# Rounding the feed-forward weights from a turned layout, in two stages instead of one

## The reference, cut to what matters

```python
x = x + _L0_xattn_ref(_layernorm(x, axis=-1), ctx_4096, ...)   # 16 heads of 96, 4 key/value heads, 4352 keys
x = x + _L0_attn_ref(_layernorm(x, axis=-1), ...)
x = x + _L0_ffn_ref(_layernorm(x, axis=-1), ...)
x = x + _L1_xattn_ref(_layernorm(x, axis=-1), ctx_4096, ctx_4096, ...)
x = x + _L1_attn_ref(_layernorm(x, axis=-1), ...)
x = x + _L1_ffn_ref(_layernorm(x, axis=-1), ...)

def _quant_w(W):
    ws = jnp.max(jnp.abs(W), axis=1, keepdims=True) / QMAX
    ws = jnp.maximum(ws, 1e-08)
    Wq = jnp.clip(jnp.round(W / ws), -QMAX, QMAX)
    return (Wq, ws)
...
Wgq, wsg = _quant_w(Wg)     # 2752 x 1024
Wuq, wsu = _quant_w(Wu)     # 2752 x 1024
gate = jnp.einsum('td,id->ti', q, Wgq) * s * wsg.T
up = jnp.einsum('td,id->ti', q, Wuq) * s * wsu.T
h = jax.nn.silu(gate) * up
q2, s2 = _quant_act(h)
Wdq, wsd = _quant_w(Wd)     # 1024 x 2752
out = jnp.einsum('ti,di->td', q2, Wdq) * s2 * wsd.T
```

## Time and profile before

| | us |
|---|---|
| median of 3 runs | 2063.93 (2061.02 to 2064.44) |
| the profiled execution | 2066.84 |
| its span, first to last instruction | 2065.5 |
| latent stage in it | 0 to about 650 |
| cross stage in it | 655 to about 1096 |
| busy over the span | PE 93%, DVE 62%, ACT 42%, POOL 27% |

### The profile page before, as it was taken

How to read it: one execution, slowest core, us unless ns; L and a number is a source line. 1 busy time by engine, 2 the same in 40 slices (tenths; PEclk the granted TensorE clock), 3 DMA queues, 4 the chain that set the end, 5 groups by cost and what they waited for, 6 DMA issues and landing times.

```text
span 2065.5 us, 29644 instructions
## 1 busy us (share of the span) xinstructions
PE 1924.9 (93%) x11932; PEld 1415.2 (69%) x11932; DVE 1279.1 (62%) x1612; ACT 859.0 (42%) x1409; POOL 547.5 (27%) x264
## 2 busy tenths in 40 slices
PE   7899999999997999999999898879999999978988
PEld 5799999999996777878777787533333333366854
DVE  3445454545453778888976764767777775256465
ACT  2211111111111666666565353036676767645431
POOL 0000000000000455555430000136777777610000
PEclk9999999999998999999999999989999999999999
DMA  5533334343324765665644433743343421036033
GB/s 178 175 101 115 109 106 118 98 124 94 84 80 134 212 206 175 203 198 198 220 142 137 162 122 82 168 123 80 73 91 73 87 70 27 21 127 239 1 125 143
DMA packets 154824, 259.30 MB, mean 126 GB/s; under 512 B 36493, under 2 KB 102337, under 8 KB 147521
## 3 DMA queue, kind: packets, MB, share of 16 engines
q1 hardware_dynamic: 154689, 257.42, 41.8%
HBM read 192.39 MB, written 61.76 MB: 123 GB/s over the span
## 4 chain that ended last, share of the span: by engine, by line
PE 82%; DVE 10%; ACT 3%; issue 2%; DMA 2%; SPq 1%; POOL 0%; ACTq 0%; DVEq 0%
PE psum L490 11%; PE psum L1732 7%; PE psum L1749 5%; PE psum L471 4%; PE psum L473 4%; PE psum L472 4%; PE psum L458 4%; PE psum L295 3%; PE psum L296 3%; PE psum L297 3%; PE psum L1765 3%; DVE top L1923 3%; PE psum L438 3%; PE psum L831 3%; PE psum L846 3%; PE psum L833 3%
## 5 line engine op out<-in xcount | busy, mean ns | idle before, releaser
L1923 DVE TENSOR_REDUCE top<-psum 128x4 f32<-128x2048 f32 (+1 forms) x146 | 294.0, 2025 | 97.8 <-PE psum L1713 97.6
L1993 POOL TENSOR_TENSOR added<-probs_f 128x1024 f32<-128x1024 f32 x126 | 299.3, 2377 | 166.3 <-ACT probs_f L1848 118.7
L1848 ACT ACTIVATE probs_f<-psum 128x512 f32<-128x512 f32 x512 | 278.5, 594 | 136.6 <-PE psum L1732 124.1
L623 DVE TENSOR_REDUCE top<-psum 128x2 f32<-128x512 f32 x272 | 186.5, 691 | 198.1 <-PE psum L458 197.9
L922 DVE TENSOR_TENSOR probs_low<-probs,probs_high 128x1024 fp32r<-128x1024 f32 x136 | 196.0, 1445 | 78.8 <-ACT probs L885 78.7
L884 ACT ACTIVATE probs_high<-psum 128x1024 fp32r<-128x1024 f32 x136 | 139.8, 1028 | 165.4 <-PE psum L833 151.8
L1732 PE MATMUL psum<-q_rows,k_rows 97*128 97x512 f32 x512 | 196.0, 457 | 2.7 <-DMA q_rows<-t_high 2.0
L1732 PEld LDWEIGHTS psum<-q_rows,k_rows 97*128 97x128 f32 x512 | 80.0, 189 | 171.8 <-ACT probs_f L1848 161.5
L471 PE MATMUL psum<-c_high,w_high 128*128 128x256 f32 (+1 forms) x672 | 190.7, 284 | 3.2 <-issue 3.2
L472 PE MATMUL psum<-c_low,w_high 128*128 128x256 f32 (+1 forms) x672 | 190.4, 283 | 0.0
L473 PE MATMUL psum<-c_high,w_low 128*128 128x256 f32 (+1 forms) x672 | 190.4, 283 | 0.0
(11 more groups left out here) (363 smaller groups left out, 3814.7 us busy)
## 6 DMA issues: line engine op xcount, KB each, us to landing
wf_rows<-in_ffn_w_dram SPq DMA_DIRECT2D x42, 512.0 KB, 4.1
staged<-in_ctxT_dram SPq DMA_DIRECT2D x32, 512.0 KB, 4.7
k_four<-k_high SPq DMA_DIRECT2D x128, 128.0 KB, 3.3
wf_rows<-in_ffn_w_dram SPq DMA_DIRECT2D x8, 1376.0 KB, 7.6
q_dram<-wf_turned SPq DMA_DIRECT2D x42, 256.0 KB, 2.3
gate_up<-q_dram SPq DMA_DIRECT2D x10, 1024.0 KB, 8.1
value_high<-v_high SPq DMA_DIRECT2D x32, 256.0 KB, 3.7
value_low<-v_low SPq DMA_DIRECT2D x32, 256.0 KB, 4.8
```

Source lines behind the costliest of these rows:

```text
L623: dve.tensor_reduce(top0[:, r0:r0 + 2, n], psum[:, bank, :].rearrange("p (i n) -> p i n", i=2), AX_X, ALU.max).then_inc(*b.bank_read.up())
L1848: act.activation(probs[:, n % 6, half * BANK:(half + 1) * BANK], psum[:, half, :], ACT.Exp, scale=scale).then_inc(*f.exped.up())
L1923: dve.tensor_reduce(top1[:, first:end, t, chunk], psum[:, MAXIMA + first:MAXIMA + end, :], AX_X, ALU.max).then_inc(*f.max_read.up())
L1993: pool.tensor_tensor(added[pair % 4][:], probs[:, n % 6, :], probs[:, (n + 1) % 6, :], ALU.add).then_inc(*f.added.up())
```

## The change

The host program hands over the three feed-forward weights a second time, turned (`ffn_t0`, `ffn_t1`, `ffn_t2`). A new class `Whole` rounds them: the rows are still loaded in the old layout to find their largest values (`dve_find_top`), the inverse scales are sent to DRAM and read back as a row on all partitions (`inverse_dram`), and the turned weights are loaded in pairs of 128-row tiles of at most 512 columns, multiplied by the inverse scales on POOL, moved by the rounding constant on ScalarE (latent stage) or VectorE (cross stage), moved back into bf16 on ScalarE, and spilled. Nothing is transposed on the matrix engine.

The work is in two places. In the latent stage: 6 blocks, 40 row pieces and 38 pairs, set at four slots per chunk in chunks 1 to 15 (`SLOTS`; a "find" place for VectorE and a "settle" place for ScalarE and SP in each; a pair is loaded at slot r + 15, multiplied when it is there, shifted and rounded at slot r + 17, spilled at slot r + 18). In the cross stage: 8 blocks, 28 row pieces and 32 pairs, one slot in three steps from step 9 on (`slots`).

To make room in SBUF the latent stage keeps `q_low` in the tiles of the second context chunk, sends it to `q_low_dram`, and reads it back before chunk 16; ScalarE may start the high part of chunk 1 only when it has been sent (`b.q_low_sent`). `xnT` goes to `xnT_dram` and comes back as the last context chunk. From context piece 2 on only two of the `staged` tiles take the context. The feed-forward block reads the rounded weights in their new layouts with plain slices.

```diff
     def act_chunk(n, half):
         high = c_high[n % 2][:, 4 * half:4 * half + 4, :]
+        if n == 1:
+            act.wait_ge(*b.q_low_sent.at(32))
         if n >= 2:
             act.wait_ge(*b.made.at(made_by[n - 2]))
...
+            whole = Whole(whole_b, [(0, 0), (1, 0), (2, 0), (0, 1), (1, 1), (2, 1)], rows, turned, inverses)
+            LAG = 16
+            SLOTS = {("mm", 0, 0, 0): "find", ("mm", 0, 1, 1): "settle", ("mm", 1, 0, 0): "find",
+                     ("mm", 1, 1, 1): "settle", ("vmm", 0, 0, 0): "find", ("vmm", 0, 0, 3): "settle",
+                     ("vmm", 1, 0, 0): "find", ("vmm", 1, 0, 3): "settle"}
...
     # scalar engine, latent stage
+                        if what == "settle" and 0 <= i - LAG - 1 < len(whole.pairs):
+                            whole.act_shift(i - LAG - 1)
+                            whole.act_round(i - LAG - 1)
     # SP, latent stage, ahead of the chunks
+                    loaded = place["c", 3] + 1
+                    for n in range(loaded):
+                        load(n)
+                    for i, part in enumerate(q_low_parts):
+                        sp.wait_ge(*b.q_split.at(8 * i + 8))
+                        sp.dma_start(q_low_dram[:, i * 8 * T:(i + 1) * 8 * T],
+                                     part[0:HD0, :].bitcast(F32)).then_inc(*b.q_low_sent.up(16))
...
+            def pool_multiply(self, r):
+                block, z, i, m = self.pairs[r]
+                width = self.width_of(z, i)
+                tile, wt_in, _, times = self.tile(r)
+                both = tile[:, 0:2 * width].rearrange("p (z n) -> p z n", z=2)
+                if m == 0:
+                    pool.wait_ge(*self.q.inverse_in.at(16 * (block + 1)))
+                pool.wait_ge(*wt_in.at(16 * (times + 1)))
+                pool.tensor_tensor(both, both,
+                                   self.inverses[block % 2][:, 0:width].unsqueeze(1).broadcast_to([P, 2, width]),
+                                   ALU.mult).then_inc(*self.q.scaled.up())
+            def act_shift(self, r):
+                z = self.width_of(*self.pairs[r][1:3])
+                tile = self.tile(r)[0]
+                act.wait_ge(*self.q.scaled.at(r + 1))
+                act.activation(tile[:, 0:2 * z], tile[:, 0:2 * z], ACT.Copy, bias=ROUND).then_inc(*self.q.shifted.up())
...
+            whole = Whole(whole_c, [(z, i) for i in range(2, chunks) for z in range(2)], ...)
+            LAG = 7
+            slots = {9 + 3 * i: i for i in range(len(whole.pairs) + LAG + 2)}
...
-                pe.wait_ge(*s.ident_b_set.at(1))
                 scores(0)
                 scores(1)
                 for n in range(STEPS):
                     if n + 2 < STEPS:
                         scores(n + 2)
                     weigh(n)
-                    for what, m, first, last in quant[n]:
-                        if what == "turn":
-                            turn(m, first, last)
     # vector engine, cross stage
+                    if n in slots:
+                        u = slots[n]
+                        if u < len(whole.tops):
+                            whole.dve_find_top(u)
+                            if u in whole.top_end:
+                                whole.dve_scales(whole.top_end.index(u))
+                    elif n - 1 in slots:
+                        u = slots[n - 1] - LAG - 1
+                        if 0 <= u < len(whole.pairs):
+                            whole.dve_shift(u)
     # scalar engine, cross stage
+                    if n - 2 in slots:
+                        u = slots[n - 2] - LAG - 1
+                        if 0 <= u < len(whole.pairs):
+                            whole.act_round(u)
```

More of the change, by code:

```diff
@@ L140, in build @@
         c = flags("Cross", CROSS, new("cross", CROSS))
+        whole_b = flags("Whole", WHOLE, new("whole", WHOLE))
         first_causal = flags("Causal", CAUSAL, new("causal", CAUSAL))
@@ L363, in latent_stage @@
             phase = ExitStack()
+            rows = [sb(phase, f"wf_rows{i}", [P, D]) for i in range(3)]
+            turned = [sb(phase, "wf_turned", [P, 2 * BANK])]
             xnT = sb(phase, "xnT_ab", [P, KT, T])
@@ L420, in chunk_steps @@
                     maximum()
-                return steps
+                if n == 0 or n == LATENTS:
+                    return steps
+                slotted, slot = [], (n - 1) * len(SLOTS) // 2
+                for step in steps:
+                    if step in SLOTS:
+                        slotted.append((SLOTS[step], slot, 0, 0))
+                        slot += SLOTS[step] == "settle"
+                    slotted.append(step)
+                return slotted
             per_chunk = 3 + 2 + 4 * G0 * TT // 2
@@ L684, in load @@
-                        source = a["ctxT"][i // 2, :, i % 2 * 4 * CH:(i % 2 + 1) * 4 * CH]
-                    sp.dma_start(destination, source).then_inc(*stage_in[n % 4].up(16))
-                loaded = place["c", 5] + 1
-                for n in range(loaded):
-                    load(n)
-                read = 0
-                for n in range(NCH):
+                        destination = tile[:, 0:4 * CH]
+                        source = (xnT_dram[i % 2] if i // 2 == LATENTS
+                                  else a["ctxT"][i // 2, :, i % 2 * 4 * CH:(i % 2 + 1) * 4 * CH])
@@ L692, in sync_program @@
+                for n in some:
                     latents = n == LATENTS
@@ L1085, in sync_program @@
                         m += 1
-                    for what, i, first, last in quant[n]:
-                        if what == "turn" and (last > 16 or i < 2 * FT):
-                            spill(i)
-                        elif what == "settle" and i + 2 < NQ:
-                            load_rows(i + 2)
             gpsimd_program()
@@ L1097, in cross_stage @@
             phase.close()
+            for sent in whole.spilled:
+                dve.wait_ge(*sent.now())
+            dve.wait_ge(*whole_c.inverse_in.now())
+        whole_c = follow("Whole", WHOLE, whole_b)
         cross_stage()
@@ L2146, in gate_and_up @@
                     if t == 0:
-                        so_far = sum(64 if m == chunks - 1 else 32 for m in range(i % 3, i + 1, 3))
-                        pe.wait_ge(*chunk_in[i % 3].at(so_far))
+                        pe.wait_ge(*chunk_in[i % 3].at(32 * (i // 3 + 1)))
                     if i == 0:
```

447 lines of the change are left out of this document (234 added, 213 removed).

## The result

The changed kernel takes 2054.93 us (median of 5 runs, 2044.02 to 2057.24) and the kernel before 2064.44 us in the same comparison: a ratio of 0.994 (95%: 0.9923 to 0.9958). It is faster, as forecast, by 10 us and not by 35.

A forecast was written before the change was run, and what follows sets the result against it. PE, busy 93% of the span, was taken as the bound. Terms -22.9 - 13.1 - 3.8 - 2 + 6.5 = -35.3 us took the profiled 2066.84 to 2031.5, as a median about 2029 us; range 2016 to 2052.

The forecast's parts named there:

- The transposes: Cross stage: transposes lie bare on PE and go; 22.9 us saved at short blocks and 13.1 us at long blocks.
- the wait at the start of the cross stage: Cross stage start: VectorE's wait for a row load, with PE behind it, goes; 3.8 us saved, bounds 0 and 3.8.
- the head changes: Cross stage, three key/value head changes: VectorE has less beside its normalising and catches up sooner; 2 us saved.
- The wait added at chunk 0: Latent stage start: ScalarE waits until q_low is in DRAM, PE stands 4.4 us; 6.5 us lost with the slower clock.
- Latent stage at nothing: Latent stage: added maxima on VectorE, copies on ScalarE and transfers fit beside PE's 34 us chunks; cost 0.
- rival C: Latent stage: weights reach POOL late, key and value copies and PE wait, so the kernel is slower; chance 0.10.
- Feed-forward at 0: Feed-forward block: last gate and up chunk takes 16 matmuls of 192 columns, equal columns in all; cost 0.
- Rivals B and D: B: chunk 0 wait hidden, head changes gain more, 2019, chance 0.08. D: transposes were hidden, no gain, chance 0.02.
- Work added to the cross stage, costed at nothing: Cross stage: added ScalarE, VectorE and POOL work is covered by PE's 8.3 us per three-step slot; cost 0.
- the slack: Cross stage step: a split held at most 2.38 us by POOL hides in 2.7 us before PE needs it; cost 0.
- at most the same 1.2: Cross stage: VectorE's addition of the rounding constant, once per three steps, takes no longer than a maximum, 1.2 us.
- Rival A: Cross stage: VectorE, POOL and ScalarE become the bound through held splits; 10 to 29 us, so 2039 to 2058; chance 0.14.

The follow-up runs named there:

- e4: Changed kernel with POOL's product of the first context attention replaced by one-column memsets, part of the weights left unscaled: 2041.11 us, ratio 0.9902.
- e3: Changed kernel with ScalarE's rounding in the cross stage one step later in its queue: 2043.66 us, ratio 0.9911.
- e13: Changed kernel with the tile w_parts made 256 bytes per partition in place of 96: 2048.88 us, ratio 0.9918.
- e14: The changed kernel itself, without an edit, measured in a second comparison: 2048.12 us, ratio 0.9915.
- e5: Changed kernel with w_parts reserved inside the first attention's stack, behind q_high, in place of ahead of it: 2041.55 us, ratio 0.9886.
- e9: Not the reference's work: TensorE alone, matmul triples over 8 places each of stationary and moving tile, no transfers or other engines; span 248.1 us.

## Why the prediction was wrong

**Right.** *The transposes* and *the wait at the start of the cross stage*: outside the disturbed places every step is 2.77 us. In e4, where nothing disturbs, step 0 to 135 falls by 45.1 us (427.1 to 382.0): 39.8 for these two terms, and 5.3 at the head changes, for which 2 was forecast. *The wait added at chunk 0*: `q_low` landed at 89.7 us against "about 90", PE stood 5.3 us against 4.4, with the clock at 0.50 behind it, and chunk 1 came 5.9 us later, against 6.5. Some luck is in that: this execution began chunk 0 1.3 us earlier than the one before, so the wait itself cost 7.2 us. *Latent stage at nothing*: chunks of 33.9 us, rival C did not happen. *Feed-forward at 0*: 73.9 us from its first matmul to the end before, 73.3 after. Rivals B and D did not happen either.

**Wrong: "Work added to the cross stage, costed at nothing".** The stretch missed its forecast by 13.9 us. 10 are the disturbed steps outside the head changes, the rest lies around the head changes, where two executions of one kernel differ by 5 us (17.0 and 12.1). The step that failed is the slack. The prediction set a block of at most 2.38 us against 2.2 + 0.5 = 2.7 us of slack in front of PE and took nothing. The blocks were sized about right (splits of up to 3.4 us in place of 1.2), and no more frequent than before. But the 2.7 us were read in the kernel before, where ScalarE's exponentials were on time. Now ScalarE has a rounding in its queue that waits up to 3.3 us for VectorE's shift (outside the head changes), and the exponentials of the next step stand behind it. ScalarE's 7.2 of 8.3 us was read as cover and has room for 1.1 us of waiting, so the exponentials, and the splits that follow them, come late, and a held split meets no slack. e3 shows it: the holds stay, the order in ScalarE's queue changes, and some 7.5 us come back. A second sentence failed with it: the shift was put at "at most the same 1.2". It takes 0.69 us alone; beside POOL's product it took 2.9 us, three times in the changed kernel. The product also is not always 2.38 us; it took 4.07 where it was held up in turn. The Trainium skill (SBUF - State Buffer, section "Who interferes with whom") names `tensor_scalar` among the VectorE instructions that can take the ports that it shares with GpSimd for a whole instruction, and fp32 in SBUF is what the shift works on; the 2.88 us above and the 0.69 us of e4 agree. I had weighed that section for the split and not for the instruction that the change adds. Rival A had the price, 10 to 29 us, and "a late rounding" in its mechanism, but a chance of only 0.14.

**Wrong: a term that is missing.** The stretch behind the cross stage was taken as unchanged, by 0 us. It lost 9.1, of which 6.1 are the place of the tiles (the time lines of e13 against e14); the other 3 are not explained. Nothing in the rows of before shows this. What would have pointed to it is that the change reserves a tile ahead of all others.

**In the working.** The prediction reads the last line of the earlier trace rows one column off: "VectorE 330, ScalarE 349, POOL 269" are the weight loads, VectorE and ScalarE; VectorE has 349 us, ScalarE 269 and POOL 212. No term of the sum uses them. The bounds of its terms, added up, give about 2019 to 2046 and not 2018 to 2039. The "some 2 us" of any transfer are 2.8 by the row that it names (5.7 less 2.9). And part of the miss is spread between comparisons: e14's 2048.12 us lies inside the stated range, 2016 to 2052, where the first comparison's 2054.93 does not.

**Not settled.** Why e5's runs gained more than its paces; what decides in which executions POOL's products fall on splits and shifts, and so the 8 us between two profiles of the same kernel; the 3 us behind the cross stage; why the operands' places matter to TensorE.

## What to carry to other kernels

An instruction put into a queue can cost the time that it waits, not only the time it runs: for each one ask what stands behind it, and put it behind the work that has no slack. A slack read in the kernel before holds only while the engines that feed it are as early as they were there. Where work for POOL comes beside VectorE, check each of VectorE's instructions for the hold, new ones first. And when matmuls slow down that a change did not touch, compare the addresses of their operands: reserve new tiles behind the others, or in multiples of 256 bytes.

## What the hardware showed

The pace of 128x512 fp32r matmuls depends on where their operands lie within 256 bytes per partition: 0.2269 us from start to start in the causal projections of before, 0.2333 with the stationary tiles 32 bytes further on, 0.2345 at 96, 0.2326 at 128, 0.2269 again at 256. TensorE alone shows 0.227 to 0.235 (e9). The steps of the cross stage, 2.76 to 2.77 us in all these kernels, hardly changed with it.

VectorE's fp32 shift of 128x1024 in SBUF takes 0.69 us alone and 2.88 us when it starts in a running product of POOL (e4; the changed kernel); the split, 1.22 us alone, takes 2.3 to 3.4 us there.
